# The tables of a one-hot lookup made one part each, and the four engines' orders rewritten

## The reference

```
e = stack([tbl_f[ids[:, f]] for f in range(26)], axis=1)            # 512 x 26 x 128
combined = concatenate([dense[:, None, :], e], axis=1)              # 512 x 27 x 128
pairs = einsum('bnd,bmd->bnm', combined, combined)[:, TRIU_I, TRIU_J]
h = concatenate([dense, pairs, dense], axis=1)                      # 512 x 607
h = maximum(h @ W_top1 + b_top1, 0)                                 # 512 x 512
h = maximum(h @ W_top2 + b_top2, 0)                                 # 512 x 256
y = h @ W_top3
```

## Time and profile before

| | us |
|---|---|
| median of three runs | 109.44 (109.06 to 109.80) |
| the profiled execution | 109.33 |
| its span, first to last instruction | 107.4 |
| busy: TensorE, VectorE, ScalarE, GpSimd | 98.3, 86.0, 64.4, 64.5 |

### The profile page before, as it was taken

How to read it: one execution, slowest core, us unless ns; L and a number is a source line. 1 busy time by engine, 2 the same in 40 slices (tenths; PEclk the granted TensorE clock), 3 DMA queues, 4 the chain that set the end, 5 groups by cost and what they waited for, 6 DMA issues and landing times.

```text
span 107.4 us, 3972 instructions
## 1 busy us (share of the span) xinstructions
PE 98.3 (92%) x1657; PEld 80.4 (75%) x1657; DVE 86.0 (80%) x255; ACT 64.4 (60%) x110; POOL 64.5 (60%) x68
## 2 busy tenths in 40 slices
PE   5969897997999899998999999999999997999991
PEld 2337576764766788877899887999798866998890
DVE  4799999999999999999999999999572436078121
ACT  5699989999999997809989474846300040001210
POOL 3577778777777778777777777777777700000000
PEclk9999999999999999999999999999999999999999
DMA  2999985747567847999782852112222110000000
GB/s 59 319 288 329 396 266 169 206 135 228 168 173 236 247 146 219 329 326 315 252 279 63 227 167 55 49 49 55 55 58 67 52 31 6 0 6 0 0 6 1
DMA packets 10575, 16.19 MB, mean 151 GB/s; under 512 B 2352, under 2 KB 6478, under 8 KB 10558
## 3 DMA queue, kind: packets, MB, share of 16 engines
q1 hardware_dynamic: 8398, 11.62, 34.0%
q0 software_dynamic: 2016, 4.13, 13.3%
q10 hardware_dynamic: 144, 0.19, 0.5%
HBM read 15.94 MB, written 0.00 MB: 148 GB/s over the span
## 4 chain that ended last, share of the span: by engine, by line
POOL 57%; issue 18%; PE 15%; DMA 6%; POOLq 1%; DVE 1%; DVEq 0%
POOL rows_sb L530 57%; PE h_ps L675 3%; DMA rows_sb<-in_tbl,ids_sb 3%; PE h_ps L650 3%; DMA ids_sb<-in_ids 2%; PE gram_ps L594 2%; PE h_ps L619 1%; PE turn_ps L650 1%; POOLq L293 1%; PE gram_ps L650 1%; PE turn_ps L619 1%; PE h_ps L658 1%; PE gram_ps L611 1%; PE turn_ps L594 1%; PE place_ps L611 0%
## 5 line engine op out<-in xcount | busy, mean ns | idle before, releaser
L530 POOL DMA_INDIRECT rows_sb<-in_tbl,ids_sb x63 | 63.6, 1009 | 20.9 <-issue 18.9
L571 PE MATMUL turn_ps<-onehot_sb,high_sb 128*128 128x512 f32 (+2 forms) x118 | 41.9, 367 | 3.5 <-DVE low_sb L807 1.4
L798 DVE TENSOR_SCALAR_CACHE_REDUCE onehot_sb<-lookup_ids_sb,first_sb 128x256 fp32r<-128x256 int16 (+2 forms) x79 | 43.6, 598 | 0.0
L572 PE MATMUL turn_ps<-onehot_sb,low_sb 128*128 128x512 f32 (+2 forms) x118 | 38.9, 342 | 0.0
L571 PEld LDWEIGHTS turn_ps<-onehot_sb,high_sb 128*128 128x128 f32 x118 | 22.2, 188 | 9.5 <-DVE low_sb L807 2.4
L572 PEld LDWEIGHTS turn_ps<-onehot_sb,low_sb 128*128 128x128 f32 x118 | 22.3, 189 | 1.6
L739 ACT ACTIVATE onehot_sb<-lookup_ids_sb,first_sb 128x512 fp32r<-128x512 int16 (+2 forms) x31 | 18.8, 621 | 2.3 <-PE turn_ps L572 2.2
L807 DVE TENSOR_TENSOR low_sb<-table_sb,high_sb 128x640 fp32r<-128x640 f32 (+1 forms) x26 | 19.4, 757 | 0.0
L729 ACT CAST high_sb<-table_sb 128x640 fp32r<-128x640 f32 (+1 forms) x26 | 17.0, 672 | 3.0 <-PE turn_ps L572 2.8
L594 PE MATMUL gram_ps<-feats 128*32 128x27 f32 x960 | 12.8, 196 | 1.1 <-DVE feats L701 0.4
L747 ACT ACTIVATE onehot_sb<-onehot_sb 128x768 fp32r<-128x768 f32 (+4 forms) x13 | 13.6, 1049 | 0.1
(11 more groups left out here) (53 smaller groups left out, 74.2 us busy)
## 6 DMA issues: line engine op xcount, KB each, us to landing
table_sb<-in_tbl SPq DMA_DIRECT2D x13, 256.0 KB, 3.5
table_sb<-in_tbl SPq DMA_DIRECT2D x7, 320.0 KB, 3.6
lookup_ids_sb<-in_lookup_ids SPq DMA_DIRECT2D x12, 128.0 KB, 2.4
table_sb<-in_tbl SPq DMA_DIRECT2D x6, 192.0 KB
rows_sb<-in_tbl,ids_sb POOLq DMA_INDIRECT x63, 3.3
w1p_sb<-in_w_pairs SPq DMA_DIRECT2D x1, 768.0 KB
w1d_sb<-in_w_dense SPq DMA_DIRECT2D x1, 512.0 KB, 6.3
w_sb<-in_w SPq DMA_DIRECT2D x1, 512.0 KB, 6.0
```

Source lines behind the costliest of these rows:

```text
L530: pool.indirect_dma_start(out=rows_sb[:, GATHERS.index((tile, slot)), :], out_offset=None, in_=tables[f], in_offset=bass.IndirectOffsetOnAxis(
L571: nc.tensor.matmul(bank, high_sb[0:rows, u % 2, c, :], picked, start=c == 0, stop=False)
L572: nc.tensor.matmul(bank, low_sb[0:rows, u % 2, c, :], picked, start=False, stop=c == CHUNKS[u] - 1).then_inc(chunk_used, 1)
L798: nc.vector.tensor_scalar(onehots(u, [c])[:, 0, :], lookup_ids_at(u), row_ids_sb[:, row:row + 1], None, ALU.is_equal, ALU.add, accum_out=m ...
```

## The change

Tables 1 to 12 become one part each, and table 0 keeps its two. A table of one part has one transfer for all its full chunks and one for the last chunk, and one cast over 1024 or 1280 columns. `low u 0` is now two subtractions in a row, each over half of the part, of which the second alone counts up the semaphore; for table 0 each half of the table is thereby subtracted in two pieces of 256 columns. TensorE waits for the whole table's remainder ahead of its first chunk.

All four orders are new. In the changed file each table of orders stands twice; the later definition is the one that holds, and the lines below show it.

```diff
 def table_parts(u):
-    return [range(0, CHUNKS[u] // 2), range(CHUNKS[u] // 2, CHUNKS[u])]
+    return [range(0, CHUNKS[u] // 2), range(CHUNKS[u] // 2, CHUNKS[u])] if u == 0 else [range(0, CHUNKS[u])]
 
 def dve_chunks(u):
-    first, second = table_parts(u)
-    return [first, range(second.start, CHUNKS[u] - ACT_CHUNKS[u])]
+    return [range(part.start, min(part.stop, CHUNKS[u] - ACT_CHUNKS[u])) for part in table_parts(u)]
...
 DVE_ORDER = """
-    onehot 0 0:4; low 0 0; low 0 1; onehot 0 4; low 1 0; onehot 0 5; onehot 1 0:5; low 1 1; onehot 2 0:4; low 2
...
+    onehot 0 0:4; low 0 0; onehot 0 4:6; onehot 1 0; low 0 1; onehot 1 1; low 1 0; onehot 1 2:5; low 2 0; onehot
+    2 0:6; onehot 3 0; low 3 0; onehot 3 1:5; onehot 4 0:2; low 4 0; onehot 4 2:6; onehot 5 0; low 5 0; onehot 5
...
 SP_ORDER = """
-    ids; table 0; id; table 1; table 2; dn; w1d; table 3; table 4; table 5; table 6; mask; table 7; table 8;
-    table 9; w1p; table 10; sm; w2; table 11; table 12
+    ids; table 0; id; table 1; table 2; table 3; table 4; sm; table 5; table 6; dn; table 7; mask; table 8; w1d;
+    table 9; w2; table 10; table 11; w1p; table 12
...
-        table_loaded = [[sem(f"table_loaded{u}_{part}") for part in range(2)] for u in range(LOOKUPS)]
+        table_loaded = [[sem(f"table_loaded{u}_{part}") for part in range(len(table_parts(u)))]
+                        for u in range(LOOKUPS)]
...
-                act.wait_ge(table_loaded[u][part], 16 * (part + 1))
+                act.wait_ge(table_loaded[u][part], 32 if part == len(table_parts(u)) - 1 else 16)
...
             def low(u, part):
                 at, chunks = u % TABLE_BUFS, table_parts(u)[part]
-                c = slice(chunks.start, chunks.stop)
                 dve.wait_ge(high_split, done("act", "cast", u, part))
-                nc.vector.tensor_tensor(low_sb[:, u % 2, c, :], table_sb[:, at, c, :],
-                                        high_sb[:, u % 2, c, :].bitcast(FP32), ALU.subtract).then_inc(low_split, 1)
+                middle = (chunks.start + chunks.stop) // 2
+                for c in (slice(chunks.start, middle), slice(middle, chunks.stop)):
+                    last = nc.vector.tensor_tensor(low_sb[:, u % 2, c, :], table_sb[:, at, c, :],
+                                                   high_sb[:, u % 2, c, :].bitcast(FP32), ALU.subtract)
+                last.then_inc(low_split, 1)
```

More of the change, by code:

```diff
@@ L235 @@
+    layer1 3 1 2; layer1 3 2 3; layer1 3 3 4; layer2 3 0; layer2 3 1
 """
 ACT_ORDER = """
-    distance 0 6; cast 0 0; distance 0 7; cast 0 1; distance 1 5; cast 1 0; distance 1 6; onehot 0; distance 1
-    7; onehot 1; cast 1 1; cast 2 0; distance 2 6; copy lookup 0; cast 2 1; distance 2 7; dense; cast 3 0;
-    onehot 2; cast 3 1; distance 3 5:7; copy turn 0 0; copy lookup 1; distance 3 7; copy turn 0 1; copy lookup
-    2; cast 4 0; onehot 3; distance 4 6:8; cast 4 1; cast 5 0; copy lookup 3; distance 5 5; cast 5 1; copy turn
@@ L247 @@
[L247 to L250 removed]
+    distance 0 6:8; cast 0 0; cast 0 1; onehot 0; distance 1 5:7; cast 1 0; distance 1 7; onehot 1; distance 2
+    6:8; cast 2 0; copy lookup 0; onehot 2; copy turn 0 0; distance 3 5:7; copy turn 0 1; cast 3 0; copy lookup
@@ new lines @@
+    1; distance 3 7; dense; copy lookup 2; onehot 3; distance 4 6; cast 4 0; distance 4 7; onehot 4; cast 5 0;
+    copy lookup 3; copy turn 0 2; distance 5 5:8; onehot 5; copy lookup 4; distance 6 8; copy turn 0 3; cast 6
+    0; twin 0; distance 6 9; copy lookup 5; copy turn 0 4; cast 7 0; distance 7 7; onehot 6; distance 7 8:10;
+    cast 8 0; copy lookup 6; distance 8 8:10; copy turn 1 1; onehot 7; twin 1; twin 2; copy lookup 7; onehot 8;
+    cast 9 0; distance 9 7:9; place 0 0 32; twin 3; distance 9 9; copy lookup 8; distance 10 8; onehot 9;
@@ L251 @@
+    distance 10 9; onehot 10; copy turn 1 3; cast 10 0; cast 11 0; copy lookup 9; distance 11 7:10; copy lookup
+    10; distance 12 7; copy turn 2 1; distance 12 8; cast 12 0; distance 12 9; onehot 11; copy lookup 11; onehot
+    12; copy turn 2 3; copy lookup 12; place 1 0 32; copy turn 3 1; copy turn 3 3; place 2 0 32; place 3 0 16;
+    place 3 16 32; relu1 3 0 1; relu1 3 2 3
 """
 DVE_ORDER = """
-    onehot 0 0:4; low 0 0; low 0 1; onehot 0 4; low 1 0; onehot 0 5; onehot 1 0:5; low 1 1; onehot 2 0:4; low 2
@@ L260 @@
[L260 to L264 removed]
+    onehot 0 0:4; low 0 0; onehot 0 4; low 0 1; onehot 0 5; onehot 1 0:2; low 1 0; onehot 1 2:5; onehot 2 0:2;
@@ L265 @@
+    copy turn 2 0; onehot 11 5:7; onehot 12 0:3; low 12 0; merge 1 0 16; onehot 12 3; copy turn 2 2; onehot 12
+    4:7; merge 1 16 32; place 1 0 32; layer3 0; copy turn 3 0; relu1 1 0 4; merge 2 0 16; merge 2 16 32; copy
+    turn 3 2; place 2 0 32; copy turn 3 4; layer3 1; merge 3 0 16; relu1 2 0 4; merge 3 16 24; merge 3 24 32;
+    layer3 2; place 3 16 32; relu1 3 1 2; relu1 3 3 4; layer3 3
 """
 SP_ORDER = """
-    ids; table 0; id; table 1; table 2; dn; w1d; table 3; table 4; table 5; table 6; mask; table 7; table 8;
@@ L269, with steps @@
-    table 9; w1p; table 10; sm; w2; table 11; table 12
+    ids; table 0; id; table 1; table 2; table 3; dn; table 4; table 5; w1p; table 6; w1d; table 7; table 8; sm;
+    w2; table 9; mask; table 10; table 11; table 12
+"""
+def steps(table):
+    for entry in table.split(";"):
+        kind, *which = entry.split()
+        which = [w if w.isalpha() else [int(v) for v in w.split(":")] for w in which]
+        if which and len(which[-1]) == 2:
+            yield from ((kind, *(w[0] for w in which[:-1]), c) for c in range(*which[-1]))
+        else:
+            yield (kind, *(w if isinstance(w, str) else w[0] for w in which))
```

89 lines of the change are left out of this document (55 added, 34 removed).

## The result

| | before | after |
|---|---|---|
| median | 109.39 us (109.06 to 109.80, 4 runs) | 111.23 us (110.64 to 112.01, 4 runs) |
| the profiled execution, its span | 109.33, 107.4 | 111.24, 109.4 |
| busy: TensorE, VectorE, ScalarE, GpSimd | 98.3, 86.0, 64.4, 64.5 | 99.4, 86.5, 63.1, 64.5 |

The ratio is 1.017, with a 95% interval of 1.0098 to 1.0242: the change makes the kernel slower by about 1.8 us. The forecast was 110.0 with a range to 111.4, so the time lies inside, near the upper end, and 1.2 us beside the likeliest value. The granted clock is 1.00 in both profiled executions.

What follows compares the result with a forecast made beforehand. Two chains were taken to bind together: the last gather, and TensorE's work ahead of `turn 3 4`. Terms 1.8 + 0.2 - 0.8 - 0.4 - 0.2 = +0.6 on 109.33 gave 110.0 us, range 108.6 to 111.4.

Steps and rivals of the forecast that it cites:

- The sum: Whole kernel: 1.8 + 0.2 - 0.8 - 0.4 - 0.2 = +0.6 us on the profiled 109.33, giving 110.0 us.
- 1.8 + 0.2: TensorE around table 9: 1.8 us behind by waiting for the whole table, 0.2 more as `turn 1 4` waits for a bank.
- 0.8 + 0.4: Waits a later TensorE no longer meets: 0.8 us for copies and a merge (57.5 to 75.5), 0.4 at the last turns.
- three signs of being wrong: Last turn waiting for its gather, idle time before `low 1` or `low 2`, last landing over 1 us off 88.5.
- This needs VectorE to run without a gap, as it does before: VectorE's row up to table 9: condition for chunk 6 of table 9 being ready at 57.2 us.
- the position of 52.7 us: VectorE behind the merges of tile 0: 52.13 + 0.40 (one more one-hot) + 0.17 (two more subtractions) = 52.7.
- The tail, -0.2: Kernel end: `layer3 1` leaves the last copies' way, tile 3's first merge runs under `layer1 2`; -0.2 us (0 to -0.4).
- The gathers: GpSimd: a gather starting inside a subtraction waits for its end; subtractions' total as before, last landing 88.5, give or take 1 us.
- Rival 1: Gathers bind alone: TensorE makes up its 1.8 us, the end is last landing plus tail, 109.1 us; chance 0.22.
- Rival 2: At `low 1` and `low 2` a whole table's cast comes late and VectorE stalls: 111.0 us if 1.4 late; chance 0.19.
- Rival 3: Two subtractions in a row act as one lock and shut gathers out: some 4 us more, 113.5 us; chance 0.03.
- Rival 4: Faster: gathers miss several subtractions and TensorE isn't behind; -1.5, 107.9 us; chance 0.12.

Runs made afterwards that it cites:

- experiment 1: The changed kernel with `gram 0 1 1` moved ahead of `turn 1 3` on TensorE: 110.26 us, ratio 1.0061 to the kernel before.
- experiment 6: The changed kernel with `gram 0 1 1` ahead of `turn 1 3`, and `turn 1 3` moved behind `place 0`: 109.78 us, ratio 1.0037 to the kernel before.
- experiment 2: The changed kernel's new orders, with tables 1 to 12 in two parts as before the change: 110.61 us, ratio 1.0089 to the kernel before.
- experiment 8: The kernel before, with the new orders of TensorE, ScalarE and VectorE from `place 1` on: 109.61 us, ratio 1.0034.
- experiment 3: The change without its orders (one part a table, orders from before): 111.95, 115.83, 117.24 and 118.35 us, no ratio.
- experiment 4: One part a table with the orders from before the change, run once more: 115.77 us, ratio 1.0508 to the kernel before.
- experiments 9 to 11: More subtraction pieces: in the changed kernel, the kernel before, the changed kernel with `turn 1 3` behind `place 0`: 181.41, 180.68, 180.81 us (kernel before 180.1).

## Why the prediction was right, and where not

**The sum, without the step that failed: right.** Experiments 1 and 6, in which VectorE has no gap, give +0.6% and +0.4%, that is 110.26 - 109.61 = 0.65 and 109.78 - 109.34 = 0.44 us beside the forecast's +0.6. The place of each step is in experiment 6 within 0.1 us for VectorE and 0.4 for TensorE. Term by term its trace has TensorE 2.3 us behind at the start of table 10 (62.90 against 60.64), where the forecast has 1.8 + 0.2, and 1.2 us made up from there to the last turn (26.80 against 27.96 us), where it has 0.8 + 0.4.

**That 111.23 lies inside the range is in part luck.** The upper end of 111.4 was set with late casts in mind and with the terms at their bounds. Neither happened; a loss that the prediction did not have took their place. Its three signs of being wrong stayed away too (no wait for the last gather, no idle time at `low 1` or `low 2`, last landing at 88.5), while what it expected to see was off by 1.7 to 2.0 us: the copy of `place 0` at 57.65 and not near 56, `lookup 9` at 56.52 and not 54.7, `layer1 0` at 60.99 and not 59. Two slips change nothing: the upper bounds of its terms add up to 109.33 + 1.8 + 0.6 = 111.7 and not 111.5, and layer 2 of tile 0 stands ahead of `place 1` whole, not by half, in both orders.

**"This needs VectorE to run without a gap, as it does before": failed.** It is the sentence on which the position of 52.7 us rests, and it was taken over from the kernel before without asking what the new order puts in front of the merges. In the kernel before, the gram that the second merge needs is done at 46.5 us, 5.5 us ahead of `turn 1 3` (TensorE's timeline before):

```profile
45.74 0.79 PE L594 MATMUL gram_ps<-feats 128*32 128x27 f32 x64
...
52.03 0.66 PE L555 MATMUL turn_ps<-ident_sb,rows_sb 128*128 128x128 f32 x4
```

In the new order it stands behind it, and `turn 1 3` waits for a gather. That gather starts 1.33 us later than before (46.09 against 44.76): 0.13 because the first gather starts later (3.63 against 3.50) and 1.20 because more of the stretches fall ahead of it. It also takes 5.13 us to land, where the page's median is 3.5. Of the 1.75 us that VectorE stands idle, some 1.1 us is this wait and the rest, as experiment 2 shows, the place of `gram 0 1 1` alone. What the gap costs is about 1.65 us at the copy of `place 0` and, by experiment 1, some 1.0 to 1.2 us of the end. The forecast had asked about late gathers only at the last turn, and about idle VectorE only at `low 1` and `low 2`.

**What was made up.** Forecast -0.8 and -0.4, measured -1.7 in the changed kernel (26.22 against 27.96 us). Between `layer1 0` and the last turns TensorE idles 0.1 us in all, so these waits did go, as the forecast said; its last turn doesn't wait for its gather either. The forecast counted idle time alone and had no term for the 1.0 us by which the same products are shorter.

**The tail, -0.2.** -0.1 in the trace after (18.0 against 18.1), -0.1 to -0.2 in that of experiment 8. No run's median shows it; experiment 8, which has all orders from `place 1` on, loses 0.3 us by the median, of which the profiled execution has nothing.

**The gathers.** Last start 85.12 against 85.03, sum of the stretches 4.0 as before: the forecast's "as before" held for the sum, and hid that its distribution along the way matters when something stands behind a gather in the middle.

**Rival 1 (gathers alone, 109.1)** fell: no wait for the last gather. **Rival 2 (whole-table cast late)** did not happen in the changed kernel: VectorE is contiguous there, though its cast 1 waited 0.44 us for the load. Its mechanism is real, as experiment 3 shows (2.23 and 2.45 us; in experiment 4, the same kernel, 0.74 and 0.61); the new orders keep clear of it. **Rival 3 (the pair is one lock)** fell: made really into one instruction, the same work moves the last gather by 1.7 us and the end by 1.8. **Rival 4** fell: TensorE is behind, and the stretches still sum to 4.0 us.

**What of the change costs.** The orders: +1.0 us with the parts undone (experiment 2, 0.7 to 1.3). Without `gram 0 1 1` behind `turn 1 3` 0.4 to 0.7 us are left, which is the forecast's sum. Whether the whole-table parts add the rest in the changed kernel is not told apart: 1.0089 and 1.0170 have intervals that overlap, and in the traces VectorE's idle time is 0.96 and 1.75 us. They do cost with the old orders (experiments 3 and 4), which give them no lead. No version tried beats the kernel before; the nearest is experiment 6.

Left open: whether shorter subtractions bring the end forward, as the times of experiments 9 to 11 are disturbed; why the one gather takes 5.1 us to land (the load of table 10 is issued at 45.51 to 46.78, right beside it, but before, the transfers' share was higher in the same stretch, and there the gathers from 46.01 and 47.26 took 5.5 and 4.9 us, with nothing waiting behind them); and the pause in `gram 3` of experiments 3 and 4.

## What to carry to other kernels

When an order is rewritten, look for each consumer at everything that now stands ahead of its producer on the producer's engine, and ask of each of those what it waits for: a step put ahead of one that feeds another engine delays that engine, by its own work and by whatever it waits for, and a late transfer becomes idle time two engines away. A total that stays the same (all stretches 4.0 us, last gather at 85.1) doesn't say that the transfers in the middle arrive when they did. And a claim that an engine has no gap is a claim on the old order, to be worked out again for the new one.
